# A quantised residual adapter stack on one core: W2's blocks land where G's blocks lay, and four of its eight remainders are made by ScalarE and an accumulating transfer

## What is computed

```python
x = x + quantise(x)                      # 8 thresholds, a step and a zero point for each
x = x + x @ weight[ids_a[b]].T           # W1: one of 8 matrices 1024x1024 per batch
x = x + x @ W.T + 0.5 * (x @ lora_A[ids_b[b]]) @ lora_B_w.T     # W2 is this W, the same for all batches
x = x + (x @ B[ids_a[b]].T) @ A[ids_a[b]].T                     # rank 16
```

## Time and profile before

| | us |
|---|---|
| median of 3 executions | 479.95 (479.84 to 480.12) |
| the profiled execution | 479.68 |
| its span, first to last instruction | 477.9 |
| PE busy | 463.7 (97%) |
| DVE busy | 411.1 (86%) |
| ACT busy | 358.1 (75%) |
| POOL busy | 82.6 (17%) |

### The profile page before, as it was taken

One profiled execution on the slowest core, in us unless ns is written; L12 is line 12 of the kernel. 1 busy time (PEld: TensorE's weight loads), 2 busy tenths in 40 slices (PEclk: granted clock), 3 DMA queues, 4 the chain that ended last, 5 costly groups with the idle time before them and its releaser, 6 DMA issues.

```text
span 477.9 us, 8194 instructions
## 1 busy us (share of the span) xinstructions
PE 463.7 (97%) x3184; PEld 424.8 (89%) x3184; DVE 411.1 (86%) x481; ACT 358.1 (75%) x383; POOL 82.6 (17%) x74
## 2 busy tenths in 40 slices
PE   3999989999999999999999999999999999999997
PEld 3979779898999989898999989898999989898995
DVE  5999899999999899997999799997999799997220
ACT  6969958777978879786968779786978879784011
POOL 1074001500106001420006001320017001320000
PEclk9999999999999999999999999999999999999999
DMA  8997317632457223921357123931347133831002
GB/s 282 407 414 260 123 34 281 176 103 82 137 163 217 82 67 113 342 62 60 132 174 211 55 94 99 334 84 60 132 145 241 44 104 99 307 69 46 0 1 88
DMA packets 25895, 70.75 MB, mean 148 GB/s; under 512 B 3472, under 2 KB 13968, under 8 KB 21776
## 3 DMA queue, kind: packets, MB, share of 16 engines
q1 hardware_dynamic: 17808, 66.81, 37.5%
q0 software_dynamic: 8064, 3.67, 6.4%
HBM read 60.51 MB, written 9.96 MB: 147 GB/s over the span
## 4 chain that ended last, share of the span: by engine, by line
PE 86%; ACT 5%; SPq 3%; DMA 2%; DVE 2%; issue 1%; POOL 1%; DVEq 0%; POOLq 0%
PE x_bank L610 45%; PE acc L635 35%; PE x_bank L623 3%; DMA w1b<-w 2%; PE acc L647 2%; PE acc L645 2%; ACT mask L346 1%; ACT tq L331 1%; ACT w2h L402 1%; DVE y L462 1%; SPq L198 1%; SPq L197 1%; POOL w1b L295 0%; SPq L207 0%; ACT outb L406 0%
## 5 line engine op out<-in xcount | busy, mean ns | idle before, releaser
L610 PEld LDWEIGHTS x_bank<-x,w1b 128*128 128x128 f32 x2048 | 232.1, 192 | 3.6 <-issue 2.0
L610 PE MATMUL x_bank<-x,w1b 128*128 128x128 f32 x2048 | 232.5, 275 | 0.7 <-DVE x L475 0.6
L331 ACT ACTIVATE tq<-xin,magic,rdelta 128x1024 f32<-128x1024 f32 x128 | 157.0, 1234 | 5.3 <-DVE y L450 3.6
L346 ACT ACTIVATE mask<-absx,negtop 128x1024 bf16<-128x1024 f32 x112 | 128.3, 1145 | 36.2 <-DVE y L462 35.6
L462 DVE COPY_PREDICATED y<-mask,uq 128x1024 f32<-128x1024 int16 x112 | 150.8, 1346 | 2.5 <-DVE y L462 0.5
L307 POOL DMA_DIRECT2D w1b<-ident x56 | 66.2, 1456 | 304.8 <-DMA w1b<-w 304.5
L441 DVE TENSOR_SCALAR tq<-tq,par 128x1024 f32<-128x1024 f32 x128 | 97.6, 763 | 0.7 <-ACT tq L331 0.4
L450 DVE TENSOR_SCALAR uq<-tq,ylow,yhigh 128x1024 f32<-128x1024 f32 x112 | 91.7, 819 | 0.2 <-DVE y L462 0.2
L635 PE MATMUL acc<-w2h,x2h 128*128 128x512 f32 x256 | 80.9, 393 | 1.1 <-DVE x2l L481 1.1
L635 PE MATMUL acc<-w2l,x2h 128*128 128x512 f32 x256 | 79.3, 391 | 1.4 <-DVE y L462 1.4
L635 PE MATMUL acc<-w2h,x2l 128*128 128x512 f32 x256 | 79.9, 389 | 0.0
(11 more groups left out here) (58 smaller groups left out, 224.9 us busy)
## 6 DMA issues: line engine op xcount, KB each, us to landing
w1b<-w SPq DMA_DIRECT2D x32, 1024.0 KB, 6.7
xin<-x SPq DMA_DIRECT2D x16, 512.0 KB, 4.3
out<-outb SPq DMA_DIRECT2D x14, 512.0 KB, 2.7
w2g<-w2n SPq DMA_DIRECT2D x4, 1024.0 KB, 10.7
w1b<-ident POOLq DMA_DIRECT2D x56, 64.0 KB, 4.4
ring<-w2t SPq DMA_DIRECT2D x6, 512.0 KB, 9.5
ua<-e_dram SPq DMA_DIRECT2D x16, 128.0 KB, 2.5
ua<-w2t SPq DMA_DIRECT2D x2, 512.0 KB, 8.8
```

What stands on the lines that cost most here:

```text
L331: nc.scalar.activation(tq[:, n % TQ, :], flat(xin, c % UN), ACT.Identity, bias=magic[:, 0:1], scale=rdelta[:, g:g + 1]).then_inc(t_ready, 1)
L346: nc.scalar.activation(mask[:, n % MK, :], absx[:, :], ACT.Relu, bias=negtop[:, g:g + 1], scale=1.0).then_inc(mask_ready, 1)
L610: last = nc.tensor.matmul(x2_bank[2 * t + i][:, o % HALF * P:(o % HALF + 1) * P], w1b[:, o, at:at + P], x1[:, t, k, :], start=(o % HALF == ...
```

## The change

The ring is gone. Each block k of W2 is loaded into w2g's own block k as soon as PE has read that block for G (g_tiles at k+1), all eight before the first transfer of G's table. The buffers are laid out so that w2l0 (remainders 0 to 3) is w2g's first half: DVE subtracts in place. Remainders 4 to 7 lie apart, in w2l1: ACT writes the negative of w2h there, and POOL issues an accumulating transfer that adds W2's block out of w2g. u_hh lies on w2g's block 4 and therefore waits for the first of these transfers. The four subtractions of DVE move from steps 10 to 13 to steps 18 to 21, where they take the place of the other four. Two E copies move from steps 12 and 13 to 18 and 19, the first V from 14 to 19 (its remainder from 18 to 20), the first U from 21 and 22 to 23 and 24, and one x2l of DVE from step 15 to 16. PE does all LOW products after the W1 products of unit 1.

```diff
+        w2l = [sb("w2l0", [P, HALF, D], f32r)]
+        u_hh = sb("u_hh", [P, D], f32r)
+        w2_rest = sb("w2_rest", [P, HALF - 1, D])
+        w2l.append(sb("w2l1", [P, HALF, D], f32r))
...
             def load_w2(k):
-                if k >= ST:
-                    sp.wait_ge(w2l_ready, k - ST + 1)
-                sp.dma_start(stage[k % ST], w2t[k, :, :]).then_inc(stage_in[k % ST], 16)
+                sp.wait_ge(g_tiles, k + 1)
+                sp.dma_start(w2g[:, k, :], w2t[k, :, :]).then_inc(w2_in[k], 16)
...
             for j in range(PAIRS):
                 load_w1(a0, j)
                 load_w2(j)
+            for k in range(PAIRS, KT):
+                load_w2(k)
             sp.wait_ge(g_ready, 2)
...
-            load_w2(4)
-            load_w2(5)
             sp.wait_ge(g_out, 16)
             load_v(a0, lab0)
-            load_w2(6)
-            load_w2(7)
...
-            sp.wait_ge(w2l_ready, ST + 1)
+            sp.wait_ge(pads, 4)
             load_u(a0)
...
+            nc.gpsimd.memset(ua[:, :], 0.0).then_inc(pads, 1)
...
+            for k in range(HALF, KT):
+                pool.wait_ge(w2h_negated, k - HALF + 1)
+                nc.gpsimd.dma_start(w2l[1][:, k - HALF, :], w2g[:, k, :].bitcast(f32r), accum_op=ALU.add) \
+                    .then_inc(w2l_in[k - HALF], 16)
...
-        ACT_E = (12, 13, 13, 14)
-        ACT_W2, DVE_W2 = (9, 10, 11, 12, 13, 14, 15, 16), (10, 11, 12, 13, 18, 19, 20, 21)
+        ACT_E = (18, 19, 13, 14)
+        ACT_W2, DVE_W2 = (9, 10, 11, 12, 13, 14, 15, 16), (18, 19, 20, 21)
+        ACT_W2N = (18, 19, 20, 21)
-        ACT_X2, DVE_X2 = (14, 16), (13, 15)
-        ACT_V, DVE_V, DVE_V0 = 14, 15, 18
-        ACT_U, DVE_U, DVE_U0 = 21, 23, 26
+        ACT_X2, DVE_X2, DVE_X20 = (14, 16), (13, 15), (13, 16)
+        ACT_V, DVE_V, ACT_V0, DVE_V0 = 14, 15, 19, 20
+        ACT_U, DVE_U, ACT_U0, DVE_U0 = 21, 23, 23, 26
...
+                else:
+                    act.wait_ge(w2l_in[0], 16)
                 if part == 0:
                     nc.scalar.activation(u_hh[:, :], ua[:, :], ACT.Copy).then_inc(uh_ready, 1)
...
+                if n in ACT_W2N:
+                    i = ACT_W2N.index(n)
+                    nc.scalar.activation(w2l[1][:, i, :], w2h[:, HALF + i, :].bitcast(f32), ACT.Copy, scale=-1.0) \
+                        .then_inc(w2h_negated, 1)
...
-                    nc.vector.tensor_tensor(w2l[:, k, :], stage[k % ST], w2h[:, k, :].bitcast(f32),
+                    nc.vector.tensor_tensor(w2l[0][:, k, :], w2g[:, k, :], w2h[:, k, :].bitcast(f32),
...
+                if first:
+                    pe.wait_ge(g_ready, 2)
+                    pe.wait_ge(x2l_ready, 1)
+                    for k in range(HALF):
+                        pe.wait_ge(w2h_ready, k + 1)
+                        product(0, k, HIGH)
+                    pe.wait_ge(x2h_ready, 2)
+                    for k in range(HALF, KT):
+                        pe.wait_ge(w2h_ready, k + 1)
+                        product(0, k, HIGH[0:1])
+                    pe.wait_ge(x2l_ready, 2)
+                    for k in range(HALF, KT):
+                        product(0, k, HIGH[1:2])
+                    pe.wait_ge(e_ready, EH)
...
-                if first:
-                    pe.wait_ge(y_ready, selections(2 * G - 1))
-                    for k in range(HALF):
-                        pe.wait_ge(w2l_ready, k + 1)
-                        product(0, k, LOW)
-                    pe.wait_ge(e_ready, 2 * EH)
                 pe.wait_ge(x1_ready, UN * b + 2)
                 w1_x1(b, 1, range(OT))
                 if first:
-                    for k in range(HALF, KT):
-                        pe.wait_ge(w2l_ready, k + 1)
+                    for k in range(KT):
+                        if k < HALF:
+                            pe.wait_ge(w2l_ready, k + 1)
+                        else:
+                            pe.wait_ge(w2l_in[k - HALF], 16)
                         product(0, k, LOW)
```

More of the change, by code:

```diff
@@ L67, in quantised_residual_adapter_stack @@
             pass
-        w2l = sb("w2l", [P, KT, D], f32r)
-        ring = sb("ring", [P, ST - 1, D])
+        w2l = [sb("w2l0", [P, HALF, D], f32r)]
+        u_hh = sb("u_hh", [P, D], f32r)
+        w2_rest = sb("w2_rest", [P, HALF - 1, D])
+        w2l.append(sb("w2l1", [P, HALF, D], f32r))
         absx = sb("absx", [P, CH])
@@ L83, in quantised_residual_adapter_stack @@
         ua = sb("ua", [P, D])
-        u_hh = sb("u_hh", [P, D], f32r)
         u_hl = sb("u_hl", [P, D], f32r)
@@ L95, in quantised_residual_adapter_stack @@
         ycut = uq[:, 1, :]
-        stage = [ua[:, :]] + [ring[:, i, :] for i in range(ST - 1)]
         a3s = outb[:, 0, :]
@@ L115, in quantised_residual_adapter_stack @@
         w2g_in = [sem(f"w2g_in{j}") for j in range(KT // 2)]
-        stage_in = [sem(f"stage_in{c}") for c in range(ST)]
+        w2_in = [sem(f"w2_in{k}") for k in range(KT)]
         u_in = sem("u_in")
@@ L157, in quantised_residual_adapter_stack @@
         w2l_ready = sem("w2l_ready")
+        w2h_negated = sem("w2h_negated")
+        w2l_in = [sem(f"w2l_in{i}") for i in range(KT - HALF)]
         block = ctx.enter_context(nc.Block())
@@ L284, in _ @@
             nc.gpsimd.memset(u_hl[:, :].bitcast(f32), 0.0).then_inc(pads, 1)
+            nc.gpsimd.memset(ua[:, :], 0.0).then_inc(pads, 1)
             pool.wait_ge(b_in, 64)
             def w2_diagonal(k):
-                pool.wait_ge(stage_in[k % ST], 16 * (k // ST + 1))
-                diag = stage[k % ST][:, k * P:(k + 1) * P]
+                pool.wait_ge(w2_in[k], 16)
+                diag = w2g[:, k, k * P:(k + 1) * P]
                 nc.gpsimd.tensor_tensor(diag, diag, eye[:, :], ALU.add).then_inc(w2_diag, 1)
@@ L362, in round_v @@
                 else:
-                    act.wait_ge(pads, 3)
+                    act.wait_ge(pads, 4)
                 nc.scalar.activation(v_hl[:, :, 0:R2], va[:, :, :], ACT.Copy).then_inc(vh_ready, 1)
@@ L401, in tables @@
                     act.wait_ge(w2_diag, k + 1)
-                    nc.scalar.activation(w2h[:, k, :], stage[k % ST], ACT.Copy).then_inc(w2h_ready, 1)
+                    nc.scalar.activation(w2h[:, k, :], w2g[:, k, :], ACT.Copy).then_inc(w2h_ready, 1)
+                if n in ACT_W2N:
+                    i = ACT_W2N.index(n)
+                    nc.scalar.activation(w2l[1][:, i, :], w2h[:, HALF + i, :].bitcast(f32), ACT.Copy, scale=-1.0) \
+                        .then_inc(w2h_negated, 1)
                 for e in range(2 * EH):
@@ L421, in _ @@
                     s = n - PER * b
-                    if s == ACT_V:
+                    if s == (ACT_V if b else ACT_V0):
                         round_v(b)
-                    if s in (ACT_U, ACT_U + 1):
-                        round_u(b, s - ACT_U)
+                    for part in range(2):
+                        if s == (ACT_U if b else ACT_U0) + part:
+                            round_u(b, part)
                     if s == ACT_LOW:
@@ L511, in tables @@
                     k = DVE_W2.index(n)
-                    if k == 0:
-                        dve.wait_ge(g_tiles, KT)
                     dve.wait_ge(w2h_ready, k + 1)
-                    nc.vector.tensor_tensor(w2l[:, k, :], stage[k % ST], w2h[:, k, :].bitcast(f32),
+                    nc.vector.tensor_tensor(w2l[0][:, k, :], w2g[:, k, :], w2h[:, k, :].bitcast(f32),
                                             ALU.subtract).then_inc(w2l_ready, 1)
@@ L557, in _ @@
                 for i in range(2):
-                    c, off = divmod(n - DVE_X2[i], G)
+                    c, off = divmod(n - (DVE_X20 if n < DVE_X2[1] + G else DVE_X2)[i], G)
                     if off == 0 and 0 <= c < UN * B:
@@ L634, in product @@
                     for h in halves:
-                        nc.tensor.matmul(acc[2 * t + h][:, :], xs[:, t, k, :], w[:, k, h * DH:(h + 1) * DH],
+                        cols = slice(h * DH, (h + 1) * DH)
+                        wk = w2h[:, k, cols] if w is w2h else w2l[k // HALF][:, k % HALF, cols]
+                        nc.tensor.matmul(acc[2 * t + h][:, :], xs[:, t, k, :], wk,
                                          start=(k == 0 and xs is x2h and w is w2h), stop=False, skip_group_check=True)
@@ L660, in batch @@
                     w1_x1(b, 0, range(U_AT, OT))
-                for k in range(KT):
-                    if k % HALF == 0:
-                        pe.wait_ge(x2l_ready, BANKS * b + k // HALF + 1)
-                    if first:
-                        if k == 0:
[L666 to L671, removed]
-                    pe.wait_ge(y_ready, selections(2 * G - 1))
-                    for k in range(HALF):
-                        pe.wait_ge(w2l_ready, k + 1)
-                        product(0, k, LOW)
-                    pe.wait_ge(e_ready, 2 * EH)
+                if first:
[14 more added lines that the diff above has]
+                    for k in range(KT):
```

(9 more changed lines are left out.)

## The result

The changed kernel takes 483.21 us (median of 6, 482.54 to 483.71) against 479.94 us of the kernel before, measured beside it (6 executions). The ratio is 1.0069, with a 95% interval of 1.0059 to 1.0079. The forecast was 479.1 us with a range to 481.5, so the sign and the range were both wrong. The profiled execution took 483.41 us with a span of 481.6 us, 3.7 us more than the span before.

The account below looks back on a forecast made before the run. PE's work plus its idle time between 51.20 and 64.17 us was taken as the bound. Terms -2.7 + 1.85 = -0.85 us took the profiled 479.68 to 478.83, 479.1 for the median; range 478.2 to 481.5.

Parts of the forecast that it names:

- x1 earlier by 2.7 us: Before unit 1's W1 products: x1 done at 61.3 us instead of 64.03, PE starting at 61.45 instead of 64.17.
- such a stall: Sign of error: ACT waiting for POOL's diagonals in steps 11 to 16, meaning loads do not land as assumed.
- (c): Rival at unit 1's last masks: ACT late, x1 gains only 1.46 us, net +0.4 us, 480.35; chance 0.12.
- (d): Rival before x1 of unit 1: all DVE relief counts, x1 4.9 us sooner, net -3.0 us, 476.9; chance 0.12.
- LOW behind x1, +1.85 us: On PE: LOW for blocks 0 to 3 moves behind unit 1's W1 products, where no time is idle, costing 1.85 us.
- The accumulating transfers, 6.6 us taken between 5.5 and 8.2: Before PE's LOW for blocks 4 to 7: landing in 6.6 us, no stall; at 8.2 us, 2.2 us of stall.
- the 7.7 us that the prediction gave it: Time for the last accumulating transfer, from the last negative's end at 71.5 us to PE's need at 79.2 us.
- The estimate of 3.2 us: Time of one POOL transfer by the Trainium skill: 2.0 us plus bytes at 436 GB/s; sum stays -0.85 us.
- The cover of SP's slide: SP's queue: x of unit 3 issued at 75.5 us, landing at 79.8, before DVE's first tq at about 84; no cost.
- The margin I named for x1 of unit 2, 1.5 us: At batch 1's start: x1 of unit 2 must be 0.85 us sooner, and holds by about 1.5 us.
- Rival (e): At batch 1's start: x1 of unit 2 stays at 93.34 us, PE waits, net 0, 479.95; chance 0.05.
- rival (b): After PE's 2.9 us pause: low clock slows W1 matmuls, net +0.95 to +2.75 us, 480.9 to 482.7; chance 0.08.

Follow-up runs that it names:

- ids_early: Changed kernel with SP reading batch 1's ids while idle after load_v, instead of between load_u and x of unit 3: 481.19 us, ratio 1.0024.
- both: Changed kernel with x of unit 3 loaded early and eight redundant matmuls in PE's pause before unit 1's W1 products: 479.83 us, ratio 1.0002.
- no_accum: Changed kernel without POOL's four accumulating transfers, so that part of the sum is not computed: 480.4 us, one execution.
- e_back_fill: Changed kernel with ACT's E copies back in steps 12 and 13 and eight redundant matmuls in PE's pause: 481.44 us, ratio 1.0033.
- x_early: Changed kernel with x of unit 3 loaded right after x1 of unit 1, ahead of E's transfers to DRAM: 481.83 us, ratio 1.0042.
- e_back: Changed kernel with ACT's two moved E copies back in steps 12 and 13: 481.41 us, ratio 1.0035.
- fill: Changed kernel with eight redundant matmuls in PE's pause before unit 1's W1 products: 483.61 us, ratio 1.0073.
- six: Changed kernel with x of unit 3 and ids early, six remainders by DVE, two LOW products in PE's pause: 479.16 us, ratio 0.9989.
- six_fill: The kernel of six with four redundant matmuls added in PE's pause: 477.59 us, ratio 0.9951 against the kernel before.

## Why the prediction was wrong, by its own steps

**x1 earlier by 2.7 us: right.** ACT was the bound up to x2h, DVE waited 3.21 us for it, and DVE's fixed chain followed: x2l at 47.34 us (46.80 was said), x1 at 61.79 (61.3). The difference is within what executions differ by: the same point lies at 61.16 us in the trace of ids_early and 61.41 in `both`, whose code is the same up to there but for the two ids or the filled pause, and at 62.02 in no_accum. Part of it is a stall of ACT, 0.51 us, for POOL's diagonal of block 3 at 40.0 us, which the traces of ids_early and `both` do not have. The prediction named such a stall as a sign that the loads do not land as it took it, and that holds here: POOL begins at 26.21 instead of 25.39 us in this trace. Why these loads come later was not tried. Rivals (c) and (d) are refuted.

**LOW behind x1, +1.85 us: right**, 1.81.

**The accumulating transfers, 6.6 us taken between 5.5 and 8.2: the place was right, the range too narrow at both ends.** The landing times of the four in the changed kernel and in e_back_fill:

```profile
DMA to landing us min/median/max: 5.1/6.7/7.1
DMA to landing us min/median/max: 4.5/5.0/9.4
```

The last of them took 7.1 us in the changed kernel, within the 7.7 us that the prediction gave it, and PE doesn't wait. In `both` it took 8.9 us and PE waits 1.21: this term of the sum, put at nothing, alone turns the forecast's -0.85 us into +0.36 there. The estimate of 3.2 us after the Trainium skill, DMA: Bandwidth & Descriptors, "Anatomy of one DMA", rests on a fit for transfers of POOL that says nothing of accumulating ones; these traces show it too low for them by 1.3 us at least (4.5 us against 3.2).

**The cover of SP's slide: the step that failed.** It was put as "landing 4.3 us later at 79.8, while DVE wants its first tq at about 84". Both halves were wrong. The load was issued at 80.47 us, not 75.5, and landed at 85.6, 5.8 us later than said. Of these, 3.9 us stand before load_u (72.36 instead of 68.5), for the most part because E's second transfer took 6.4 us instead of 3.5 beside the accumulating ones; 1.1 us came on top between load_u and this load, and 0.8 us in its own landing, 5.1 us instead of 4.3. And the need was not DVE's need of tq: ACT was ready for it at 80.9 us, and *behind* it on ACT stood mask and x2h, for which DVE was waiting from 82.0 us on. I had costed the wait by its own consumer and not by what is queued behind the waiting instruction. The margin I named for x1 of unit 2, 1.5 us, became a wait of 1.42 us on PE. Rival (e) named this place and load, but as a loss of the gain only, at a chance of 0.05; it cost 3.8 us with the clock out of the way (483.61 against 479.83).

**The clock, rival (b), 0.08: it happened** in five of the six executions of the changed kernel (mean granted clock 0.992 to 0.996, and 1.0 in the sixth, which at 483.71 us was the slowest of all). The price named was 1.8 to 3.6 us; in the four traces with a fall the W1 products show 1.6 (changed kernel, ids_early), 2.7 (x_early) and 2.9 us (e_back). The argument against it, that 1.40 us had done nothing, said nothing of 3.3 us. The warning of the Trainium skill, TensorE: Matmul & The Clock Gate, "Why this matters for your kernels", against idle gaps between bursts of matmuls agrees with this trace, where the low clock follows a pause of 3.30 us, and deserved more than 0.08. Yet in the changed kernel itself the fall explains none of the time, since `fill` removes it and wins nothing, and the changed kernel's fastest execution, 482.54 us, is the one with the lowest mean clock, 0.992.

What is shown: SP's late order comes first (x_early, ids_early and e_back each win 1.4 to 2.0 us of the 3.3), and the accumulating transfers lengthen it (no_accum, one execution). The low clock stands behind it: it costs 2.0 us once x is early (x_early against both). The wait for the last remainder stands behind both; its 1.2 to 1.8 us are read from the traces (both, e_back_fill), and no run takes it away alone.

## What to carry to other kernels

When work is moved later on one engine, follow every queue that waits for it to its end, and cost a late transfer by what stands behind the waiting instruction in its engine's order, not by the one instruction that reads it. Losses that meet at one point don't add: test them alone and together, or a real cause looks worthless. An idle stretch that a change opens on an engine in front of a wait (DVE's 3.2 us here) is the place for work that is otherwise made late or dearly elsewhere.

## What was not expected of the hardware

- The fall of the clock is a matter of the single execution. Five kernels have a pause of 3.2 to 3.4 us before W1's products (the changed one, x_early, no_accum, ids_early, e_back). In 23 of their 27 executions the mean granted clock was 0.992 to 0.996, in the other four 1.0; in the traces W1's products took 14.53 us (no_accum) to 17.40 (e_back). With 2.5 us, in `six`, it was 0.996 in six of ten. In the 25 executions of the four kernels whose pause was 1.4 us (fill, both, e_back_fill, six_fill) it was never below 0.999. That is no rule for 1.4 us: the kernel before has a pause of 1.40 us, and 3 of the 45 executions of it whose clock is on record had 0.996 (479.95, 480.11 and 482.83 us). Only the mean is known of them, not where the clock fell.
- An accumulating transfer of 512 KB between two places of the on-chip memory takes 4.5 to 9.4 us to land and slows down what runs beside it: E's second transfer took 6.4 us against 3.6 without them. It is slowed down in turn: the second and third of the four took 6.8 and 6.6 us beside E's transfers in the changed kernel, 4.8 and 4.5 in e_back, where E's had gone long before. POOL needs 0.86 to 1.01 us to issue one in the changed kernel, about as long as for one of 64 KB in the same trace, 0.88 us (two in 1.76).
- Reading two ids on SP takes 4.1 to 4.7 us of its queue (4.7 in the changed kernel, from 74.77 us, the end of load_u, to 79.51; 4.1 in the kernel before), about as long as the transfer that waits behind it needs to land.
